# Routing records in rows of 512 bytes, and five small moves, in a mixture-of-experts kernel

## The chip, the cores and the metric

The kernel runs on one core of one Trainium2 chip. The metric is the device time of one execution in microseconds (us); less is better.

## The reference

The input x (4096 tokens of 512 numbers) is first rotated: each token is seen as four quaternion parts of 128 numbers, and the reference's filter and two Hamilton products come down to one 4x4 matrix per column of 128. Then comes a mixture of experts with 8 experts, 2 chosen for each token, and a capacity of 1024 slots for each expert:

```python
logits = xf @ gate_w.T
scores = softmax(logits);  topv, topi = top_k(scores, 2);  gates = topv / sum(topv)
# loc: the running number of the token among those that chose the same expert
valid = loc < cap                                  # cap = 1024
flat_idx = where(valid, topi * cap + loc, 0)
disp = zeros(E * cap, D).at[flat_idx].add(xf * w)
h = relu(einsum('ecd,ehd->ech', disp, fc1_w) + fc1_b)     # 512 -> 2048
eo = einsum('ech,ehd->ecd', h, fc2_w) + fc2_b             # 2048 -> 512
out = x + sum over the 2 choices of gathered(eo) * gates
```

All is float32.

## The kernel before

**Engines.** The kernel is written for each engine by hand: an instruction waits on semaphores, and each engine works through its own list in order. PE multiplies, ACT (ScalarE) and DVE (VectorE) prepare operands and take results, SP issues most DMAs on the hardware queue q1, POOL (GpSimd) issues plain and indirect DMAs on the software queue q0, and the same 16 DMA engines carry both queues.

**Routing.** The first 60 us load x (8 MB) into `x_all`, compute the logits, pick the experts and number the tokens. While this goes on, SP writes `x_all` to `out` (8 DMAs of 1 MB, semaphore `out_init`), since the experts' results are later added to rows of `out`; behind them, in the same queue, it loads W1 of group 1 (`load_w1(1)`). For expert 0 and 1 the token of each slot is found on chip (`find_tokens`, `read_slots`). For all others a table in DRAM, `table_dram`, says it: one row for each of 8192 slots, of which the first two numbers count (token number + 1, and its gate). POOL clears it (L398, from the tile `zeros`) once all of x has arrived, and later `scatter_records` (L472) writes 64 indirect DMAs of 128 records, each record a row of RECORD numbers. The records lie two numbers apart in the tile `records`, so a row also carries what follows its record; only its first two numbers are read back. The table is read with 8 DMAs (L518, semaphore `table_in`), and `read_table` (L1037 to L1042) turns it into `gather_row` and `scatter_row`; POOL waits for that (`tables_ready`) before it gathers the tokens of expert 2 and of later experts. `store_x` and `gather_x` bring token rows through `slots_dram`, and `cut_x` on SP reads them back cut in 32x32 blocks for DVE's transpose (`turn_x`).

**Products.** For each expert, groups g = 0..7 (G counts them over all experts) make 256 rows of h with seven products per group, a Strassen-like scheme on 2x2 blocks: A22, A11, A12, S1 to S4 are parts of W1 (high and low part `w1c_hi`, `w1c_lo`), B11, B21, T1 to T4, B22 parts of the rotated x (`yc_hi`, `yc_lo`). Each product is 6 matmuls of 128x512 (L1303 to L1305). Its result is picked up by ACT (`s2`, `s3`: L686, L702; `h_hi`: L725) and by DVE (`keep_c22` L1080, `keep_c12` L1086). `fc2(N)` (L1328, L1332, L1336) multiplies one tile of h with one tile of W2: 4 matmuls each of high x high, low x high, high x low. The last three tiles of all go through `fc2_end` (L1349 to L1351), one output block of 128 rows after the other; each block is added to `out` by DVE (`add_rows`) and written by POOL. The trace leaves numbers out of names: `s` is `s2` or `s3`, `w_raw` is `w1_raw` or `w2_raw`, `h` is `h1`.

**Ahead of the main loop** DVE's list runs: `turn_w1(1)` (two transposes at L816, which need both tiles of W1 of group 1), `read_slots(1)`, sums, `make_scores`, `w1_low_parts(1, 0)`, and then the rotation (`rotate_ps` from L1012 on), from which it works through to the first `keep_c22`. In ACT's list of group 0, `y_high` (L611) makes the high parts of T4 and B22, and L686 takes `s2` from the bank of the product S2 x T2; the product S3 x T3 adds into that bank, so PE waits for `s2_ready`.

Of the kernel before, what the change touches and what calls it, by code (L numbers as in the profile page):

```python
# [15 lines left out]
P = 128  # L16


def program(nc, x, cond, q_right, spectral, gate_w, fc1_w, fc1_b, fc2_w, fc2_b, out):
    B, S, D = x.shape  # L20
    E, H, _ = fc1_w.shape
# [23 lines left out]
    RECORD = 16  # L45
# [34 lines left out]
    with ctx:  # L80
        def sb(name, shape, dt=F32, where=ctx):
            return where.enter_context(nc.sbuf_tensor(name, shape, dt))
# [82 lines left out]
        zeros = sb("zeros", [P, E * CAP * RECORD // P], where=early)  # L165
# [88 lines left out]
        def version(N):  # L254

            e, n = N // STEPS, N % STEPS
            return e * VERSIONS + (n if n < HT else n - KEPT)
# [22 lines left out]
        def _(sp):  # L280
# [47 lines left out]
            for e in range(E):  # L328
                last = e == E - 1
                for g in range(GROUPS):  # L330
                    G, N = e * GROUPS + g, e * STEPS + 2 * g
                    if e and not last and g == 2:
                        cut_x(4 * e + 3)
                    if e and e < E - 2 and g == 5:
                        cut_x(4 * e + 4)
                    if e and e < E - 2 and g == 6:
                        cut_x(4 * e + 5)
                    load_w2(version(N) + 3)
                    load_w2(version(N) + 4)
                    if G + 3 < E * GROUPS:  # L340
                        load_w1(G + 3)
                    if G == 3:
                        cut_x(2)
                    if G == 4:
                        cut_x(3)
                    if G == GROUPS + 1:
                        cut_x(6)
# [12 lines left out]
        def _(pool):  # L360
# [37 lines left out]
            pool.dma_start(table_dram.rearrange("(p k) a -> p (k a)", p=P), zeros[:, :]).then_inc(table_cleared, 16)  # L398
# [146 lines left out]
        def _(act):  # L545
# [130 lines left out]
            for e in range(E):  # L676
                last = e == E - 1
                for g in range(GROUPS):
                    G, N = e * GROUPS + g, e * STEPS + 2 * g
                    odd_bias = b1T[:, e * HT + 2 * g + 1:e * HT + 2 * g + 2]  # L680
                    if e and g == 0:
                        seed_c11(G)
                    act.wait_ge(p6_done, G + 1)
# [3 lines left out]
                    if G == 0:  # L687
                        y_high(0, T4, 4, y21)
                        y_high(0, B22, 0, y22)
# [506 lines left out]
        def _(pe):  # L1196
# [111 lines left out]
            def fc2(N):  # L1308
# [21 lines left out]
                for b in range(SB):  # L1330
                    blk = slice(b * P, (b + 1) * P)
                    pe.matmul(eo_s[:, b, :], h_lo[:, c, blk], w2_hi[:, w, :], start=False, stop=False, skip_group_check=True)  # L1332
                pe.wait_ge(w2_ready, v + 1)
# [5 lines left out]
            def fc2_end(N):  # L1339

                eo_s = ps[:, EO[1]:EO[1] + SB, :]
                for b in range(SB):
                    blk = slice(b * P, (b + 1) * P)
                    for n in range(N, N + 3):
                        c, w = n % 3, version(n) % 3
                        if b == 0:
                            pe.wait_ge(w2_ready, version(n) + 1)
                            pe.wait_ge(h_ready, n + 1)
                        pe.matmul(eo_s[:, b, :], h_hi[:, c, blk], w2_hi[:, w, :], start=False, stop=False, skip_group_check=True)  # L1349
                        pe.matmul(eo_s[:, b, :], h_hi[:, c, blk], w2_lo[:, w, :], start=False, stop=False, skip_group_check=True)  # L1350
                        ins = pe.matmul(eo_s[:, b, :], h_lo[:, c, blk], w2_hi[:, w, :], start=False, stop=n == N + 2,  # L1351
                                        skip_group_check=True)
                    ins.then_inc(eo_done, 1)
# [44 lines left out]
            for e in range(E):  # L1398
                p1(e * GROUPS)
                p1(e * GROUPS + 1)  # L1400
                for g in range(GROUPS):
# [37 lines left out]
                    if g:  # L1439
                        fc2(N - 1)  # L1440
                    if G == 1:
                        p1(G + 1)
# [26 lines left out]
```

## Time and profile before

| | |
|---|---|
| median of 3 runs | 1439.35 us (1426.83 to 1447.98) |
| profiled execution, its own time | 1436.52 us |
| span of its instructions | 1434.6 us |
| PE busy | 1380.1 us (96%) |
| DVE, ACT, POOL busy | 1048.5, 701.8, 328.2 us |
| mean granted TensorE clock | 0.982 |

The span runs from the first to the last instruction of the profiled execution; its own time is 1.9 us more. A busy share is a mean over all stages. DMA issues, semaphore and register instructions count as idle, other than POOL's descriptor work.

### The profile page before, as it was taken

To read this page: it belongs to the slowest core of one execution; us is meant where nothing else is said; L and a number is where in the kernel's file an instruction comes from. 1 tells how busy PE (TensorE), PEld (TensorE's weight loads), DVE (VectorE), ACT (ScalarE), POOL (GpSimd) and SP (SyncE) were. 2 spreads that over 40 slices of the span, in tenths; PEclk is the share of its full clock that TensorE was granted. 3 is DMA by queue.
4 is the path that set the end of the run, shared out by engine and by line. 5 is a ranking of instruction groups with operands and counts; after the bars stand their busy time and mean duration, and the time that the engine had idled before them with its cause. 6 is when DMAs were issued, how large, how long until landed. Compare 5 with 4: busy or idle time off the path is not lost.

```text
span 1434.6 us, 18099 instructions
## 1 busy us (share of the span) xinstructions
PE 1380.1 (96%) x6159; PEld 1128.3 (79%) x6159; DVE 1048.5 (73%) x1580; ACT 701.8 (49%) x1056; POOL 328.2 (23%) x350
## 2 busy tenths in 40 slices
PE   8689779999999999999999999999999999999997
PEld 6477558788888888888888888888888888888885
DVE  6888449686886878777796878777786878855543
ACT  5465245454465445554555454654454554644442
POOL 1377751321033001221032010221032000220021
PEclk9799889999999999999999999999999999999999
DMA  8866434786465564565555564665555533543232
GB/s 316 292 137 143 75 82 110 208 192 141 97 177 162 108 138 115 157 170 135 95 169 158 106 151 92 184 162 121 114 151 151 128 74 74 146 125 67 52 98 78
DMA packets 450029, 195.36 MB, mean 136 GB/s; under 512 B 397641, under 2 KB 401922, under 8 KB 448146
## 3 DMA queue, kind: packets, MB, share of 16 engines
q1 hardware_dynamic: 427378, 125.98, 39.2%
q0 software_dynamic: 22560, 68.23, 14.8%
q8 instruction: 49, 0.80, 0.2%
q14 instruction: 42, 0.34, 0.1%
HBM read 153.51 MB, written 40.89 MB: 136 GB/s over the span
## 4 chain that ended last, share of the span: by engine, by line
PE 91%; another core or an unknown queue 3%; DVE 2%; issue 1%; DMA 1%; ACT 1%; SPq 0%; POOL 0%; DVEq 0%; ACTq 0%; POOLq 0%
PE ps L1332 14%; PE ps L1328 14%; PE ps L1336 14%; PE ps L1303 14%; PE ps L1305 14%; PE ps L1304 14%; PE ps L1239 1%; PE ps L1319 1%; PE ps L1321 1%; PE ps L1320 1%; PE ps L1294 1%; PE ps L1219 1%; PE ps L1220 1%; POOL h L412 0%
## 5 line engine op out<-in xcount | busy, mean ns | idle before, releaser
L1303 PE MATMUL ps<-yc_hi,w1c_hi 128*128 128x512 f32 x896 | 350.7, 391 | 14.8 <-issue 9.4
L1304 PE MATMUL ps<-yc_lo,w1c_hi 128*128 128x512 f32 x896 | 349.4, 390 | 0.0
L1305 PE MATMUL ps<-yc_hi,w1c_lo 128*128 128x512 f32 x896 | 349.2, 390 | 0.0
L1332 PE MATMUL ps<-w_hi,h_lo 128*128 128x512 f32 x952 | 255.9, 390 | 5.6 <-issue 5.6
L1336 PE MATMUL ps<-w_lo,h_hi 128*128 128x512 f32 x952 | 256.1, 390 | 1.6 <-issue 1.5
L1328 PE MATMUL ps<-w_hi,h_hi 128*128 128x512 f32 x952 | 254.8, 389 | 1.7 <-issue 1.7
L1332 PEld LDWEIGHTS ps<-w_hi,h_lo 128*128 128x128 f32 x952 | 178.9, 188 | 44.1 <-issue 6.8
L1336 PEld LDWEIGHTS ps<-w_lo,h_hi 128*128 128x128 f32 x952 | 179.1, 188 | 41.5 <-issue 4.5
L1303 PEld LDWEIGHTS ps<-yc_hi,w1c_hi 128*128 128x128 f32 x896 | 168.6, 188 | 54.7 <-issue 12.8
L1328 PEld LDWEIGHTS ps<-w_hi,h_hi 128*128 128x128 f32 x952 | 178.7, 188 | 37.9 <-issue 0.9
L1305 PEld LDWEIGHTS ps<-yc_hi,w1c_lo 128*128 128x128 f32 x896 | 168.6, 188 | 35.4
L1304 PEld LDWEIGHTS ps<-yc_lo,w1c_hi 128*128 128x128 f32 x896 | 168.6, 188 | 34.7
L951 DVE TENSOR_TENSOR w_lo<-w_raw,w_hi 128x512 fp32r<-128x512 f32 x232 | 158.4, 683 | 6.1 <-ACT w_hi L603 3.2
L945 DVE TENSOR_TENSOR w1c_lo<-w1t,w1c_hi 128x1792 fp32r<-128x1792 f32 x62 | 125.6, 2026 | 30.4 <-ACT w1c_hi L596 26.4
L603 ACT ACTIVATE w_hi<-w_raw 128x512 fp32r<-128x512 f32 x232 | 143.7, 620 | 7.0 <-DMA w_raw<-in_L_ffn_fc_w 7.0
L740 ACT ACTIVATE h_hi<-h 128x512 fp32r<-128x512 f32 x128 | 80.8, 631 | 131.6 <-PE ps L1336 107.5
L1030 DVE SCALAR_TENSOR_TENSOR h_lo<-ps,h_hi 128x512 fp32r<-128x512 f32 x64 | 44.1, 688 | 122.4 <-ACT h_hi L647 119.5
L596 ACT ACTIVATE w1c_hi<-w1t 128x1792 fp32r<-128x1792 f32 x62 | 105.7, 1706 | 52.8 <-DVE w1t L829 31.6
L1030 DVE SCALAR_TENSOR_TENSOR h_lo<-h,h_hi 128x512 fp32r<-128x512 f32 x128 | 88.4, 692 | 57.0 <-ACT h_hi L740 52.0
L1080 DVE SCALAR_TENSOR_TENSOR h<-ps,b1T,s 128x512 f32<-128x512 f32 x64 | 47.8, 746 | 92.7 <-PE ps L1305 87.0
L1000 DVE SCALAR_TENSOR_TENSOR yfull<-x_turned,rot,yfull 128x512 f32<-128x512 f32 x168 | 114.9, 747 | 0.0
L430 POOL DMA_INDIRECT x_blk<-in_x,gather_row x56 | 57.0, 1019 | 226.4 <-DVE x_turned L991 183.6
(189 smaller groups left out, 1482.9 us busy)
## 6 DMA issues: line engine op xcount, KB each, us to landing
w_raw<-in_L_ffn_fc_w SPq DMA_DIRECT2D x232, 256.0 KB
w_raw<-in_L_ffn_fc_w SPq DMA_DIRECT2D x512, 64.0 KB
slots_dram<-x_blk POOLq DMA_DIRECT2D x28, 512.0 KB
x_blk<-slots_dram SPq DMA_DIRECT2D x224, 64.0 KB
out<-x_all SPq DMA_DIRECT2D x8, 1024.0 KB, 13.1
x_all<-in_x SPq DMA_DIRECT2D x6, 1024.0 KB, 12.5
b_bc<-in_L_ffn_fc_b POOLq DMA_DIRECT2D x8, 256.0 KB
x_all<-in_x SPq DMA_DIRECT2D x4, 256.0 KB, 3.9
```

The source lines that it names most:

```text
L596: act.activation(w1c_hi[:, G % 2, :, :], w1t[:, 1:8, :], ACT.Copy).then_inc(w1_hi_ready, 1)
L603: act.activation(w2_hi[:, v % 3, :], w2_raw[:, v % 3, :], ACT.Copy).then_inc(w2_hi_ready, 1)
L945: dve.tensor_tensor(w1c_lo[:, G % 2, :, :], w1t[:, 1:8, :], w1c_hi[:, G % 2, :, :].bitcast(F32), ALU.subtract).then_inc(w1_ready, 1)
L951: dve.tensor_tensor(w2_lo[:, v % 3, :], w2_raw[:, v % 3, :], w2_hi[:, v % 3, :].bitcast(F32), ALU.subtract).then_inc(w2_ready, 1)
L1000: ins = dve.scalar_tensor_tensor(y, x_turned[:, :, j, :], rot[:, i, j:j + 1], y, ALU.mult, ALU.add)
L1030: dve.scalar_tensor_tensor(h_lo[:, N % 3, :], full, 0.0, h_hi[:, N % 3, :].bitcast(F32), ALU.max, ALU.subtract).then_inc(h_ready, 1)
L1303: pe.matmul(bank, hi, yc_hi[:, y, q, :], start=first and q == 0, stop=False, skip_group_check=True)
L1304: pe.matmul(bank, hi, yc_lo[:, y, q, :], start=False, stop=False, skip_group_check=True)
L1305: ins = pe.matmul(bank, lo, yc_hi[:, y, q, :], start=False, stop=last and q == 1, skip_group_check=True)
L1328: pe.matmul(eo_s[:, b, :], h_hi[:, c, blk], w2_hi[:, w, :], start=False, stop=False, skip_group_check=True)
L1332: pe.matmul(eo_s[:, b, :], h_lo[:, c, blk], w2_hi[:, w, :], start=False, stop=False, skip_group_check=True)
L1336: ins = pe.matmul(eo_s[:, b, :], h_hi[:, c, blk], w2_lo[:, w, :], start=False, stop=False, skip_group_check=True)
```

## The change

Six things change. (1) RECORD is 128 in place of 16: a record is a row of 512 bytes, and the table has 4 MB. `zeros` keeps its size, and the clearing DMA reads it 8 times. (2) SP issues `cut_x(3)` ahead of `load_w1(7)` in group 4, not behind it. (3) ACT makes the high parts of T4 and B22 ahead of `s2` in group 0, not behind it. (4) PE does the product `p1(2)` inside `fc2(1)`, ahead of its last four matmuls. (5) `fc2_end` begins with blocks 0 and 1 of its first two tiles, and only then waits for the third. (6) The tile `records` has 112 more columns, cleared once.

```diff
-    RECORD = 16
+    RECORD = 128
...
-        zeros = sb("zeros", [P, E * CAP * RECORD // P], where=early)
+        zeros = sb("zeros", [P, E * CAP * RECORD // P // NB], where=early)
...
+                    if G == 4:
+                        cut_x(3)
                     if G + 3 < E * GROUPS:
                         load_w1(G + 3)
                     if G == 3:
                         cut_x(2)
-                    if G == 4:
-                        cut_x(3)
...
-            pool.dma_start(table_dram.rearrange("(p k) a -> p (k a)", p=P), zeros[:, :]).then_inc(table_cleared, 16)
+            pool.dma_start(table_dram.rearrange("(p r k) a -> p r (k a)", p=P, r=NB),
+                           zeros[:, :].unsqueeze(1).to_broadcast([P, NB, E * CAP * RECORD // P // NB])).then_inc(table_cleared, 16)
...
+                    if G == 0:
+                        y_high(0, T4, 4, y21)
+                        y_high(0, B22, 0, y22)
                     act.wait_ge(p6_done, G + 1)
                     if G:
                         act.wait_ge(c12_done, G)
                     act.activation(s2[:, :], running(G), ACT.Copy).then_inc(s2_ready, 1)
-                    if G == 0:
-                        y_high(0, T4, 4, y21)
-                        y_high(0, B22, 0, y22)
...
-            def fc2(N):
+            def fc2(N, between=None):
...
+                if between is not None:
+                    p1(between)
                 pe.wait_ge(w2_ready, v + 1)
...
-                for b in range(SB):
-                    blk = slice(b * P, (b + 1) * P)
-                    for n in range(N, N + 3):
-                        c, w = n % 3, version(n) % 3
-                        if b == 0:
-                            pe.wait_ge(w2_ready, version(n) + 1)
-                            pe.wait_ge(h_ready, n + 1)
...
+                for n in (N, N + 1):
+                    pe.wait_ge(w2_ready, version(n) + 1)
+                    pe.wait_ge(h_ready, n + 1)
+                    add_step(n, 0)
+                for n in (N, N + 1):
+                    add_step(n, 1)
+                pe.wait_ge(w2_ready, version(N + 2) + 1)
+                pe.wait_ge(h_ready, N + 3)
+                for b in range(2):
+                    add_step(N + 2, b).then_inc(eo_done, 1)
+                for b in range(2, SB):
+                    add_step(N, b)
+                    add_step(N + 1, b)
+                    add_step(N + 2, b).then_inc(eo_done, 1)
...
-                        fc2(N - 1)
-                    if G == 1:
-                        p1(G + 1)
+                        fc2(N - 1, 2 if G == 1 else None)
```

ACT's list in group 0, around the evacuation `s2` (L686 before, L690 now; L611 and L612 are `y_high`, L702 and L703 `s3`). Before:

```order
L611 ACTIVATE yc_hi<-yfull 128x1024
L611 ACTIVATE yc_hi<-x_turned 128x1024
L611 ACTIVATE yc_hi<-yfull 128x1024
L686 ACTIVATE s2<-ps 128x512
L611 ACTIVATE yc_hi<-yfull 128x1024 x2
L702 ACTIVATE s3<-ps 128x512
```

Now:

```order
L612 ACTIVATE yc_hi<-yfull 128x1024
L612 ACTIVATE yc_hi<-x_turned 128x1024
L612 ACTIVATE yc_hi<-yfull 128x1024 x3
L690 ACTIVATE s2<-ps 128x512
L703 ACTIVATE s3<-ps 128x512
```

The two high parts of T4 and B22 stand ahead of `s2`, which waits behind them.

PE's list at the end of group 1, the step `fc2(1)` and the product `p1(2)`. Before:

```order
L1328 MATMUL ps<-w2_hi,h_hi 128x512 x4
L1332 MATMUL ps<-w2_hi,h_lo 128x512 x4
L1336 MATMUL ps<-w2_lo,h_hi 128x512 x4
L1303 MATMUL ps<-yc_hi,w1c_hi 128x512
L1304 MATMUL ps<-yc_lo,w1c_hi 128x512
```

Now:

```order
L1329 MATMUL ps<-w2_hi,h_hi 128x512 x4
L1333 MATMUL ps<-w2_hi,h_lo 128x512 x4
L1304 MATMUL ps<-yc_hi,w1c_hi 128x512
L1305 MATMUL ps<-yc_lo,w1c_hi 128x512
L1306 MATMUL ps<-yc_hi,w1c_lo 128x512
L1304 MATMUL ps<-yc_hi,w1c_hi 128x512
L1305 MATMUL ps<-yc_lo,w1c_hi 128x512
L1306 MATMUL ps<-yc_hi,w1c_lo 128x512
L1339 MATMUL ps<-w2_lo,h_hi 128x512 x4
```

The six matmuls of `p1(2)` stand four matmuls earlier.

SP's list of DMAs in group 4, as the difference of the two lists (`x_blk` is `cut_x(3)`, `w1_raw` is W1 of group 7, in 8 DMAs each):

```order
 L268 DMA x_blk<-slots_dram 32x16x32 x8
 L307 DMA w2_raw<-in_L0_ffn_fc2_w 128x512 x2
+L268 DMA x_blk<-slots_dram 32x16x32 x8
 L268 DMA w1_raw<-in_L0_ffn_fc1_w 32x16x32 x8
-L268 DMA x_blk<-slots_dram 32x16x32 x8
 L307 DMA w2_raw<-in_L0_ffn_fc2_w 128x512 x2
```

The cut rows of x go ahead of the weights of group 7.

## Rows read from the trace of the kernel before

**Rows 1.** The page's first part: busy time of each engine, share of the span, instructions.

```profile
PE 1380.1 (96%) x6159; PEld 1128.3 (79%) x6159; DVE 1048.5 (73%) x1580; ACT 701.8 (49%) x1056; POOL 328.2 (23%) x350
```

**Rows 2.** Stretches of the span, busy us (instructions) of each engine, clock, DMA.

```profile
core 0: us, PE busy (x) PEld busy (x) DVE busy (x) ACT busy (x) POOL busy (x), PEclk, DMA share, GB/s
151.00:200.00 49.00, 28.43 (x100) 20.04 (x99) 15.90 (x27) 9.28 (x14) 38.43 (x39) 0.76 0.29 48
200.00:249.00 49.00, 49.00 (x217) 40.23 (x216) 41.60 (x65) 26.78 (x39) 9.41 (x9) 1.00 0.53 129
290.00:1415.00 1125.00, 1125.00 (x4959) 930.08 (x4958) 833.72 (x1218) 564.71 (x838) 179.89 (x179) 1.00 0.53 129
```

**Rows 3.** Timeline of PE, 158 to 190 us; in brackets the idle time before.

```profile
161.07 0.39 PE L1305 MATMUL ps<-yc_hi,w1c_lo 128*128 128x512 f32 x1
...
187.23 0.79 PE L1303 MATMUL ps<-yc_hi,w1c_hi 128*128 128x512 f32 x1 [9.09 <-issue]
```

**Rows 4.** Timeline of ACT, 158 to 200 us.

```profile
161.15 0.69 ACT L725 ACTIVATE h_hi<-ps,b1T 128x512 fp32r<-128x512 f32 x1 [4.02 <-remote]
...
186.59 0.60 ACT L686 ACTIVATE s<-ps 128x512 f32<-128x512 f32 x1 [13.07 <-remote]
```

**Rows 5.** Timeline of POOL: the first scatter, the last long row, the table.

```profile
84.39 1.03 POOL L472 DMA_INDIRECT table_dram<-records,slot_row  x1 [0.30 <-issue]
...
137.82 1.01 POOL L472 DMA_INDIRECT table_dram<-records,slot_row  x1 [0.30 <-issue]
...
192.03 7.11 POOL L518 DMA_DIRECT2D table<-table_dram  x8 [1.43 <-DMA table_dram<-records,slot_row]
```

**Rows 6.** The same view of stretches, for the DMA load ahead of the main loop.

```profile
27.00:30.00 3.00, 3.00 (x22) 2.02 (x21) 2.54 (x4) 1.95 (x4) 0.76 (x1) 1.00 0.80 220
...
33.00:54.00 21.00, 9.57 (x60) 6.26 (x59) 16.96 (x38) 11.37 (x23) 4.02 (x7) 0.76 1.02 415
...
58.50:60.00 1.50, 0.85 (x17) 0.85 (x18) 1.50 (x2) 0.00 (x0) 1.18 (x1) 0.50 0.00 0
60.00:72.00 12.00, 10.80 (x50) 7.54 (x50) 11.53 (x30) 4.93 (x10) 9.30 (x10) 0.81 0.67 192
72.00:97.00 25.00, 21.71 (x89) 17.22 (x87) 23.76 (x35) 14.76 (x21) 20.89 (x25) 0.93 0.59 139
```

**Rows 7.** Timeline of POOL: the clearing of the table.

```profile
27.24 0.76 POOL L398 DMA_DIRECT2D table_dram<-zeros  x1 [20.97 <-DMA x_all<-in_x]
```

**Rows 8.** Timeline of SP, 50 to 68 us: the loads of W1 for group 1.

```profile
43.13 13.60 SPq L268 DMA_DIRECT2D w_raw<-in_L_ffn_fc_w  x6
```

**Rows 9.** Timeline of DVE ahead of the main loop.

```profile
60.26 1.30 DVE L816 STREAM_TRANSPOSE w1t<-w_raw 128x512 f32<-128x512 f32 x2
...
65.40 10.01 DVE L1012 SCALAR_TENSOR_TENSOR yfull<-ps,rot,yfull 128x256 f32<-128x256 f32 x24 [0.20 <-issue]
...
89.46 1.21 DVE L974 TENSOR_TENSOR yfull<-yfull 128x1024 f32<-128x1024 f32 x1
```

**Rows 10.** Timeline of ACT, 90 to 94 us.

```profile
90.83 0.60 ACT L686 ACTIVATE s<-ps 128x512 f32<-128x512 f32 x1 [1.81 <-PE ps L1305]
91.33 2.00 ACT L611 ACTIVATE yc_hi<-yfull 128x1024 fp32r<-128x1024 f32 x2
```

**Rows 11.** Timeline of PE, 91 to 95 us.

```profile
91.86 0.50 PE L1303 MATMUL ps<-yc_hi,w1c_hi 128*128 128x512 f32 x1 [0.28 <-issue]
...
94.31 0.47 PE L1303 MATMUL ps<-yc_hi,w1c_hi 128*128 128x512 f32 x1 [0.78 <-ACT s L702]
```

**Rows 12.** Timeline of PE, 111 to 115 us.

```profile
111.75 1.07 PE L1336 MATMUL ps<-w_lo,h_hi 128*128 128x512 f32 x4
...
114.93 0.50 PE L1303 MATMUL ps<-yc_hi,w1c_hi 128*128 128x512 f32 x1 [0.75 <-ACT ps L640]
```

**Rows 13.** Timeline of DVE, 235 us: the table is read.

```profile
235.57 0.19 DVE L1039 TENSOR_SCALAR slot_row<-table 128x64 f32<-128x64 f32 x1
```

**Rows 14.** Timeline of PE, the last steps.

```profile
1418.85 0.50 PE L1349 MATMUL ps<-w_hi,h_hi 128*128 128x512 f32 x1 [0.69 <-DVE w_lo L951]
```

More of the change, by code:

```diff
@@ L1341, in fc2_end, with add_step @@
                 eo_s = ps[:, EO[1]:EO[1] + SB, :]
-                for b in range(SB):
-                    blk = slice(b * P, (b + 1) * P)
-                    for n in range(N, N + 3):
-                        c, w = n % 3, version(n) % 3
-                        if b == 0:
-                            pe.wait_ge(w2_ready, version(n) + 1)
-                            pe.wait_ge(h_ready, n + 1)
[L1349 to L1353, printed above, removed]
+                def add_step(n, b):
+                    c, w, blk = n % 3, version(n) % 3, slice(b * P, (b + 1) * P)
+                    pe.matmul(eo_s[:, b, :], h_hi[:, c, blk], w2_hi[:, w, :], start=False, stop=False, skip_group_check=True)
+                    pe.matmul(eo_s[:, b, :], h_hi[:, c, blk], w2_lo[:, w, :], start=False, stop=False, skip_group_check=True)
+                    return pe.matmul(eo_s[:, b, :], h_lo[:, c, blk], w2_hi[:, w, :], start=False, stop=n == N + 2,
+                                     skip_group_check=True)
+                for n in (N, N + 1):
[12 more added lines that the diff above has]
+                    add_step(N + 2, b).then_inc(eo_done, 1)
             def set_bits(banks):
```

## The prediction

> **What bounds the kernel now.** I read the page's busy shares first: PE works for 1380.1 of 1434.6 us [rows 1]. The view of stretches says where the other 54.5 us lie. From 290 to 1415 us PE is busy for all 1125 us at full granted clock, 2.4 GHz; so the main loop and the second layer have nothing to give to any change that leaves the matmuls as they are, and this one has the same matmuls. What is not PE time lies ahead of 97 us, in the last 20 us, and in one hole: from 151 to 200 us PE has 100 matmuls, where the next 49 us have 217 [rows 2]. At 49/217 = 0.226 us each, 117 missing matmuls are 26.4 us.
>
> What is the hole? Its 38.43 us of POOL work are the clue: POOL issues the scatters of records 26 to 63 one behind the other from 137.8 us, with nothing between them, and the last has landed when the table's load starts at 192.0 us [rows 5]. The DMA engines are nearly empty in the hole (share 0.29, 48 GB/s [rows 2]), so it is no lack of bandwidth. PE is late in a strange way: the last matmul of group 4's S2 product starts at 161.1 us, but ACT, which needs nothing but that product and an h row, takes it at 186.6 us; ACT's earlier wait of 4.0 us has no known releaser either, and PE then stands idle for 9.1 us for what ACT makes [rows 3, 4]. That is a slow PE, or slow news from PE, and not a wait written in the code. It begins some 15 us into the unbroken row of scatters and is over when they are. Nothing else in the program is special to that stretch. So the 64-byte scatters are my suspect, by time alone; no row shows the mechanism.
>
> **The change part by part**, against the profiled execution's own span of 1434.6 us (its own time is 1.9 us more, 1436.5, and 2.8 us under the median of 1439.35).
>
> *Rows of 512 bytes, the hole.* The number of scatters (64) and of rows in each (128) stays; the bytes of a scatter go from 8 to 64 KB. The bounds: the hole is gone (-26.4 us), or it stays as it is (0), or grows (a rival below). I take -26.4: the gathers of 2048-byte rows ahead of the loop (60 to 72 us, ten of them, as densely issued) go by with PE busy for 10.8 of 12 us [rows 6], so descriptors from POOL alone don't make a hole; what is special in the scatters is that they write small rows.
>
> The Trainium skill bears on this in "DMA: Bandwidth & Descriptors", section Specifications: a transfer under 512 B makes the DMA engine read, modify and write. By that rule the new rows shed the extra read; it doesn't say that PE would notice, and no row here shows it. The sum would be the same by it.
>
> *Rows of 512 bytes, the scatters' own load.* 56 KB more for each of 64 scatters is 3.7 MB over some 105 us, 35 GB/s beside loads that take a DMA share of 0.5 to 0.6. POOL's issue time goes by rows, not bytes (38.43 us for 39 instructions in the hole, 9.30 for 10 gathers of 2048-byte rows [rows 2, 6]), so 0, as long as the table is in time: its last load is issued at 199.1 us and DVE reads it at 235.6 [rows 5, 13]. With the hole gone DVE comes at 209, and POOL and DVE both come later by the next term; some 10 us of cover are left. If each of 64 scatters took 0.16 us longer, that would be used up; the spacing in the long row is now (190.6 - 137.8) / 38 = 1.39 us.
>
> *The clearing.* It is issued at 27.2 us [rows 7] with 4 MB in place of 0.5: 3.67 MB more, while SP's queue is full. From 33 to 54 us the DMA engines are saturated at 415 GB/s [rows 6], so everything behind is late by 3.67 MB / 415 GB/s = 8.8 us, less what was free from 27 to 30 us (share 0.80: 0.6 us), 8.2 us. What is behind: the writes of `out`, and in the same queue the 8 loads of W1 for group 1, the last of which is issued by 56.7 us and landed by 58.5 us, when DMA traffic is 0 [rows 6, 8]. Now they end at 66.7 us, and they meet the gathers of expert 0's rows (share 0.67 [rows 6]), for which I add 2 us: 68.7 us. DVE turns the second tile at 60.9 us (half of the pair of 1.30 us from 60.26) and the rotation begins 4.5 us later, at 65.4 [rows 9]. After that DVE is busy for 23.76 of the 25 us up to 97 us [rows 6], so its start sets everything: 68.7 + 4.5 = 73.2 in place of 65.4, **+8 us**. The bounds: +5 (no loss to the gathers and some more overlap) and +11 (the gathers win every turn). It would be 0 only if the 16 engines had more than 415 GB/s to give, and the rows don't show that.
>
> The logits are ahead of this: W1 of group 0 lands in the same stretch as the clearing, and DVE, in order, may lose 2 to 4 us on it near 31 us. That lies under the 8 us, since routing and W1 of group 1 meet only at `read_slots(1)`.
>
> The Trainium skill prices the same thing in "DMA: Bandwidth & Descriptors", section "Anatomy of one DMA — SWDGE (gpsimd) path": about 2.0 us plus bytes/436e3, so an estimate of 8.4 us for 3.67 MB more, where the row gives 8.8; the sum would be 0.4 us less.
>
> *ACT's order in group 0.* The high part of T4 waits for DVE's difference, done at 90.7 us [rows 9]; two high parts take 2.0 us, so `s2` starts at 92.7 in place of 90.8 [rows 10]. PE's S3 product, which waits for it, then starts at about 93.4 in place of 91.9, and A22 1.5 us later as well, in place of 94.3 [rows 11]. DVE gets the high parts earlier and saves 0.6 us that don't bind any more. PE's first step of group 1 comes **+1.2 us** later, after what it now waits for DVE. Bounds: 0 to +1.5.
>
> *p1(2) earlier.* In group 2 PE waits 0.75 us for ACT, whose step waits for `p1(2)` [rows 12]. Four matmuls earlier are 0.9 us: **-0.75**, and 0 if DVE's high parts of W1 are late.
>
> *fc2_end.* The third tile is waited for 0.69 us [rows 14]; six matmuls (1.4 us) now fill that. Block 3 is the last in both orders: **-0.7**.
>
> *cut_x(3) first.* 8 DMAs change places with 8 others. Behind them on SP are W2 loads, unchanged. W1 of group 7 comes that much later: it is issued in group 4 and turned in group 5, and a group is 66 matmuls or 14.9 us. In a full queue six such DMAs took 13.6 us [rows 8], so eight would take 18 and cost up to 3 us; the DMA engines are half free here (share 0.53 in the next stretch [rows 2]), so I take none. The cut rows come earlier, and `turn_x(3)` stands early in DVE's group 5, so without the hole the old order might have made DVE wait. So 0, between -2 and +3.
>
> The sum: -26.4 + 8 + 1.2 - 0.75 - 0.7 = -18.7 us. Span 1416.0, own time **1418 us**, 1.5% under the median.
>
> **Rivals.**
>
> *A, the forecast.* 1418 us; with the bounds of the clearing and ACT 1413 to 1422. Chance 0.56.
>
> *B, the hole stays.* It comes with the number of rows or with POOL's unbroken descriptor work, neither of which the change touches. For it: scatters run from 84.4 us [rows 5], and from there to 137.8 us, in rows of at most ten, they open no such hole, so the length of a row may be what counts and not what it writes. Against it: the gathers. 1434.6 + 8 + 1.2 - 1.45 + 1.9 = 1444 us, 0.3% over the median. Chance 0.23. A hole of half the size gives 1431 us, chance 0.08.
>
> *C, slower.* The hole comes with the bytes that small scattered rows write. Then eight times the bytes make it begin with the unbroken row at 137.8 and not at 151 us: 14 us more at the mean loss of the hole (26.4 of 39 us), so 9.5 us more; and the ten scatters in a row behind `store_x(1)`, 14 us, would show the same loss, 9.5 us again. Price: 1444 + 19 = 1463 us. It decides from the point where PE loses over 21.4 us in all to such holes (1439.35 - 1418); it passes 2% only if the table is late as well. Chance 0.08, a good half of it over 2%.
>
> *D, the clearing is hidden.* If out's writes give way instead of W1's loads, the start of the rotation moves by less than 3 us: 1410 us. Chance 0.05.
>
> **How the numbers follow.** A measurement of this kernel can tell about 2% from no change: under 1410.6 us is faster, over 1468.1 slower. A and D are mostly within; but the median of before moves by 10 us from run to run (1426.8 to 1448.0), perhaps with the length of the hole, and A's time would stand at 2% under the highest of them. So faster 0.18, same 0.75, slower 0.07. The range takes A, B, the half-size hole and D, each with the outer part of its own spread cut, and leaves out C, under 2 in 10 in all: 1406 to 1446.
>
> **What would show it.** Right: between 137 and 200 us of the new trace PE has no stretch under its full rate, and ACT's steps there have PE as releaser. The clearing: the last W1 load of group 1 at 66 to 71 us, DVE's first rotation at 71 to 76. The ACT term: `s2` of group 0 behind two high parts, PE idle ahead of S3 by about 1.8 us. The tail: no wait ahead of the last third of tiles. The forecast is wrong if the hole stays (B, C), or if the table comes late: then DVE waits at its read of the table, and POOL's next gathers with it.

## The result, and the profile after

The changed kernel took **1440.09 us** (median of 20 runs, 1433.83 to 1447.88); beside it, on the same chip, the kernel before took 1430.49 (20 runs, 1418.71 to 1447.98). The ratio is 1.008, 95% interval [1.006, 1.010]: a small loss that twenty runs can tell, where I had forecast a gain of 1.5%. Medians, here and below, are over all runs, but the ratios leave out a few runs in a slower state, so a ratio need not be the quotient of its two medians. The profiled execution of the changed kernel took 1437.52 us, span 1435.5.

First the same stretches as in [rows 2], and PE's busy share:

```profile
PE 1381.1 (96%) x6159; PEld 1128.6 (79%) x6159; DVE 1049.0 (73%) x1580; ACT 702.0 (49%) x1056; POOL 327.2 (23%) x350
```

```profile
151.00:200.00 49.00, 42.03 (x171) 32.86 (x170) 26.07 (x42) 13.60 (x19) 38.33 (x36) 0.93 0.61 137
200.00:249.00 49.00, 45.61 (x186) 35.80 (x187) 38.77 (x59) 26.57 (x39) 19.14 (x21) 0.93 0.49 108
290.00:1415.00 1125.00, 1125.00 (x4958) 930.04 (x4958) 835.33 (x1220) 565.94 (x839) 180.63 (x180) 1.00 0.54 129
```

The main loop is what it was. The hole is still there, later and shorter: over the two stretches 357 matmuls against 317, so 40 x 0.226 = 9 us less is lost. ACT's waits in it have no known releaser: for 9.56 us it waits for nothing that the trace shows, for 6.35 us for something that it doesn't know, as in [rows 4]. The hole is over when POOL's row is, as in [rows 5]. Timelines of ACT, then of POOL:

```profile
193.73 0.66 ACT L641 ACTIVATE ps<-ps,b1T 128x512 f32<-128x512 f32 x1 [9.56 <-issue]
200.74 0.69 ACT L726 ACTIVATE h_hi<-ps,b1T 128x512 fp32r<-128x512 f32 x1 [6.35 <-remote]
```

```profile
29.17 1.07 POOL L398 DMA_DIRECT2D table_dram<-zeros  x1 [22.79 <-DMA x_all<-in_x]
...
205.63 7.11 POOL L519 DMA_DIRECT2D table<-table_dram  x8 [1.55 <-DMA table_dram<-records,slot_row]
```

What the hole gives back is taken at the start. The timeline of DVE (L817 is the turn of W1, L1013 the rotation) answers to [rows 9], that of PE to the stretch ahead of it, and the page's DMA part gives the clearing's time from issue to landing, 14.4 us:

```profile
29.88 0.71 DVE L817 STREAM_TRANSPOSE w1t<-w_raw 128x512 f32<-128x512 f32 x1 [0.64 <-DMA w_raw<-in_L_ffn_fc_w]
40.88 0.71 DVE L817 STREAM_TRANSPOSE w1t<-w_raw 128x512 f32<-128x512 f32 x1 [9.12 <-DMA w_raw<-in_L_ffn_fc_w]
...
71.73 1.30 DVE L817 STREAM_TRANSPOSE w1t<-w_raw 128x512 f32<-128x512 f32 x2
76.59 10.00 DVE L1013 SCALAR_TENSOR_TENSOR yfull<-ps,rot,yfull 128x256 f32<-128x256 f32 x24
```

The second of these turns in the kernel before:

```profile
31.30 0.71 DVE L816 STREAM_TRANSPOSE w1t<-w_raw 128x512 f32<-128x512 f32 x1 [0.45 <-DMA w_raw<-in_L_ffn_fc_w]
```

```profile
42.23 0.61 PE L1220 MATMUL ps<-xT_hi,grot_hl 128*16 128x512 f32 x1 [8.03 <-DVE xT_lo L845]
```

```profile
table_dram<-zeros POOLq DMA_DIRECT2D x1, 4096.0 KB, 14.4
```

W1 of group 1 is no trouble: its turn at 71.73 has no wait. It is the second tile of W1 of group **0**, 9.12 us late, that stops DVE in the middle of cutting x for the logits; PE waits behind it for `xT_lo`, and the routing, and the rotation with it, start 11.2 us later (76.59 against 65.40). One profile of each would be thin, but the experiments below bear it out: with the clearing of 4 MB in this place the rotation starts at 76.6 to 79.6 us in four traces, with 512 KB at 65.4 to 70.1 in thirteen.

Around the first group, ACT and then PE, which answer to [rows 10, 11]:

```profile
101.76 2.01 ACT L612 ACTIVATE yc_hi<-yfull 128x1024 fp32r<-128x1024 f32 x2 [1.80 <-DVE yfull L975]
103.67 0.58 ACT L690 ACTIVATE s<-ps 128x512 f32<-128x512 f32 x1
```

```profile
104.39 0.47 PE L1304 MATMUL ps<-yc_hi,w1c_hi 128*128 128x512 f32 x1 [1.95 <-ACT s L690]
```

`s2` stands behind the two high parts, and PE waits 1.95 us for it, as drawn.

### The profile page after: what moved, and what is told of

It is laid out like the page before. It is cut to its first block, busy times and chain, and to the rows that moved or that the text cites. A ratio compares the mean times of both kernels' runs of the same rounds, so it can differ in the third digit from the quotient of the medians.

```text
span 1435.5 us, 18098 instructions
## 1 busy us (share of the span) xinstructions
PE 1381.1 (96%) x6159; PEld 1128.6 (79%) x6159; DVE 1049.0 (73%) x1580; ACT 702.0 (49%) x1056; POOL 327.2 (23%) x350
## 4 chain that ended last, share of the span: by engine, by line
PE 88%; DVE 3%; SPq 2%; another core or an unknown queue 2%; issue 2%; DMA 1%; ACT 1%; POOL 0%; DVEq 0%; ACTq 0%; POOLq 0%
PE ps L1333 14%; PE ps L1339 14%; PE ps L1329 14%; PE ps L1304 14%; PE ps L1306 13%; PE ps L1305 13%; SPq L268 2%; DMA w_raw<-in_L_ffn_fc_w 1%; PE ps L1320 1%; PE ps L1321 1%; PE ps L1322 1%; DVE yc_lo L979 0%; DVE yfull L1026 0%; DVE w_lo L952 0%
## 5 line engine op out<-in xcount | busy, mean ns | idle before, releaser
L703 ACT ACTIVATE s<-ps 128x512 f32<-128x512 f32 x64 | 38.3, 598 | 144.3 <-PE ps L1306 133.9
## 6 DMA issues: line engine op xcount, KB each, us to landing
table_dram<-zeros POOLq DMA_DIRECT2D x1, 4096.0 KB, 14.4
```

## The experiments

Kernels were measured in series: each series on one chip, with runs of the kernel before between them. The expectations call a series a call. The time of the kernel before is not the same in all of them, and that is the main finding:

```
series                   kernel before, median us (lowest to highest)
the changed kernel       1430.5 (1418.7 to 1448.0)
1: e1 to e4              1438.7 (1422.7 to 1452.4)
2: e5 to e8              1440.1 (1423.5 to 1455.1)
3: e9 to e12             1409.9 (1408.1 to 1412.6)
4: e13 to e16            1410.5 (1408.1 to 1415.3)
5: e17, e18              1430.3 (1419.3 to 1448.2)
```

Series 1, 2 and 3 ran on a chip of the same number, series 4 and 5 on two others.

### Series 1: the parts of the change, and no scatters

**e1**, the long rows and the clearing of 4 MB alone, in the kernel before:

```diff
-    RECORD = 16
+    RECORD = 128
```

> The kernel before with the 512-byte rows and the 4 MB clearing alone; all other moves undone. Theory now (clearing costs ahead of the loop, hole in the row of scatters gets shorter but stays): the second tile of W1 of group 0 lands near 41 us and DVE waits some 9 us for it, the rotation starts near 76.6 us in place of 65.4, and the whole is 0.6 to 1.0% slower than before. Rival (the slowdown comes from the moved steps of ACT, PE and SP): within 0.2% of before.

1451.44 us, 1.007 [1.004, 1.011]. Stretches (from here on of PE alone: busy us, matmuls, clock, DMA share, GB/s), and DVE:

```profile
151.00:200.00 49.00, 42.32 (x184) 1.00 0.60 139
200.00:249.00 49.00, 41.79 (x168) 0.86 0.43 90
```

```profile
44.55 0.71 DVE L817 STREAM_TRANSPOSE w1t<-w_raw 128x512 f32<-128x512 f32 x1 [11.18 <-DMA w_raw<-in_L_ffn_fc_w]
```

The hole is there with 512-byte rows, and so is DVE's wait for W1 of group 0. The whole loss of the change comes with this part.

**e2**, the other four edits alone (the changed kernel with `RECORD = 16` and the old clearing):

> The changed kernel with 64-byte rows and the clearing of 0.5 MB again, all moved steps kept. Theory: the rotation starts at 65 to 66 us; ACT's order costs 1.3 us, the product and the last steps give 1.4 us back, so within 0.2% of before, with a hole of some 20 to 27 us under the scatters as before. Rival (moves are the loss): 0.6% or more slower than before.

1440.8 us, 1.001 [0.998, 1.004]; 94 matmuls from 151 to 200 us, the hole of the kernel before.

**e3**, the kernel before with no scatter of records at all (the table stays empty, so the second layer's weights are left out):

```diff
-                for c in columns:
+                for c in ():
```

> The kernel before without its 64 scatters of records (left out: the table stays empty, so the experts from 2 on all take token 0 and add nothing to the output). Theory (POOL's scatters make the hole): PE has its full 217 or so matmuls in every 49 us from 115 to 290 us, and the time is 15 to 27 us shorter, 1.1 to 1.9% faster. Rival (the hole comes from something else at that place, such as instruction fetches or SP's loads): a hole of 15 us or more stays between 150 and 210 us and the time is within 0.5% of before.

1412.01 us, 0.981 [0.976, 0.986], and its runs lie within 3.8 us where those of the kernel before lie within 30.

```profile
151.00:200.00 49.00, 47.27 (x209) 1.00 0.44 85
200.00:249.00 49.00, 49.00 (x216) 1.00 0.60 147
```

No hole. So the scatters are needed for it, and the spread of the kernel before from run to run goes with the hole.

**e4**, the changed kernel with the clearing issued behind the gathers of expert 0's rows, and waited for ahead of the first scatter:

```diff
             gather_x0(range(2 * SB))
+            pool.dma_start(table_dram..., zeros...).then_inc(table_cleared, 16)
```

> The changed kernel with the 4 MB clearing issued behind the 8 gathers of expert 0's rows (from a tile of 512 bytes per partition read 64 times) and waited for ahead of the first scatter. Theory (the clearing's price is its place): DVE's wait for W1 of group 0 is under 1 us again, the rotation starts by 67 us, and the time is 6 to 11 us under the changed kernel's, 0 to 0.3% around or under before. Rival (the 4 MB cost the same wherever they are, since x blocks and W1 of group 2 wait for them next): within 0.2% of the changed kernel.

1448.11 us, 1.008 [1.005, 1.012]: as much as the changed kernel, so the rival holds, the 4 MB cost the same here. W1 of group 0 was in time and the rotation started at 66.3 us. What ate the gain up is not the hole alone: PE already does only 181 matmuls from 100 to 151 us, where e2 has 226, and waits 5.1 us for weights at 120.6, which e16 shows better. Its profiled execution, 1462.4 us, is the longest of its twelve runs, so the depth of the hole in it says little of the median:

```profile
100.00:151.00 51.00, 43.49 (x181) 0.97 0.76 180
151.00:200.00 49.00, 17.41 (x47) 0.64 0.29 74
```

### Series 2: what about the scatters makes the hole

**e5**, the clearing behind W1 of group 0:

```diff
+            for t in range(2):
+                pool.wait_ge(w1_in[t], 16 * W1_DMAS)
             pool.dma_start(table_dram..., zeros...).then_inc(table_cleared, 16)
```

> The changed kernel, with POOL waiting for both tiles of W1 of group 0 before it issues the clearing of 4 MB. Theory (the clearing costs only because it shares the DMA engines with W1 of group 0, which delays the logits and the rotation behind them by 11 us): DVE's turn of W1 of group 0 waits under 2 us again, the rotation starts near 66.5 us, and the time is that of the run with the moves only, 0.995 to 1.004 of before. Rival (the 4 MB cost the same wherever they lie, as when the clearing was issued behind the gathers of x0): 1.006 to 1.011, with the rotation at 66 us and a hole under the scatters that has grown to over 30 us. Second rival: the clearing then collides with W1 of group 1 (58.5 us before): DVE's turn of it waits 3 to 8 us, 1.002 to 1.005.

1447.18 us, 1.005 [1.002, 1.007]. Timelines of POOL and DVE:

```profile
67.46 0.95 POOL L415 DMA_INDIRECT h<-in_x,gather_row  x1 [14.64 <-DMA rows<-in_x,part_i]
```

```profile
68.46 0.71 DVE L819 STREAM_TRANSPOSE w1t<-w_raw 128x512 f32<-128x512 f32 x1 [8.11 <-DMA w_raw<-in_L_ffn_fc_w]
72.27 0.71 DVE L819 STREAM_TRANSPOSE w1t<-w_raw 128x512 f32<-128x512 f32 x1 [3.10 <-DMA w_raw<-in_L_ffn_fc_w]
```

The second rival: the ratio is at the upper end of its 1.002 to 1.005, and the waits, 11.2 us together, are more than its 3 to 8. The price has moved. The clearing, issued at 32.6 us, now takes 33.5 us to land; POOL waits 14.64 us for a gather of its own queue, issued at 51.7 us, and so the gathers of x0 are late; and W1 of group 1 is 11 us late. That is the path that I had predicted for the clearing where it stood.

**e6**, the last 38 scatters replaced by 38 gathers of 64-byte pieces of x into an idle tile (these records are left out):

```diff
-            scatter_records(range(26, TOPK * TJ))
+            for c in range(26, TOPK * TJ):
+                pool.indirect_dma_start(slab_rows[0][..16 elements..], None, x_pieces, ...)
```

> The kernel before, in which the last 38 scatters of records are replaced by 38 gathers of as many pieces of 64 bytes from x into an idle tile (the table then lacks these records, so the results of their tokens are left out). Theory 1 (the hole is made by POOL issuing an unbroken row of indirect DMAs, whatever they move): the stretch from 151 to 200 us still lacks over 80 of 216 matmuls, and the time stays within 0.5% of before. Theory 2 (the hole is made by what scatters alone do, writes of single small rows to memory and their completions): the stretch holds over 190 matmuls and the time is 0.978 to 0.987 of before, as without scatters.

1439.13 us, 0.999 [0.995, 1.002]:

```profile
151.00:200.00 49.00, 22.39 (x79) 0.66 0.32 45
```

Theory 1, clearly: nothing is written to DRAM in this row, and the hole is as deep as ever.

**e7**, a wait for all that was issued, ahead of every third scatter from number 30 on:

```diff
                 for c in columns:
+                    if c > 29 and c % 3 == 0:
+                        pool.wait_ge(records_out, 16 * c)
```

> The kernel before, in which POOL waits in the last row of 38 scatters, ahead of every third of them, until all that it issued have landed. Theory 1 (many indirect DMAs in flight at once delay the semaphores and transfers of the others): the row lasts 80 to 110 us in place of 53, its end near 230 us, but the hole shrinks to under 8 us, and the time is 0.982 to 0.992 of before. Theory 2 (each scatter costs the others its share, in flight or not): the lost time is the same, spread over the longer row, 0.996 to 1.004. Rival 3: the table is now late for VectorE's reading of it (235.6 us before), and the time rises to 1.005 to 1.015.

1432.52 us, 0.997 [0.994, 0.999], its runs within 4.6 us. PE's stretches, and DVE at its read of the table:

```profile
151.00:200.00 49.00, 47.29 (x209) 1.00 0.48 91
200.00:249.00 49.00, 30.65 (x127) 0.79 0.39 93
```

```profile
233.25 0.20 DVE L1041 TENSOR_SCALAR slot_row<-table 128x64 f32<-128x64 f32 x1 [18.27 <-DMA table<-table_dram]
```

The mechanisms of theory 1 and of rival 3 at once, so the time lies between their ranges: under the row PE is at its full rate, with the same scatters; but the row now ends at 223 us, and DVE waits 18.27 us for the table. One hole went and another, this one plainly written in the program, took its place.

**e8**, the last 19 scatters left out (and their records):

```diff
-            scatter_records(range(26, TOPK * TJ))
+            scatter_records(range(26, 45))
```

> The kernel before with the last 19 of 64 scatters left out (their records are missing from the table, so their tokens' results are left out too). The last row is then 19 scatters, some 25 us, from 138 to 163 us. Theory 1 (a hole opens only once a row has lasted some 25 us, here at 161 us, and lasts until the row ends): no hole, the stretch from 151 to 200 us holds over 200 matmuls, time 0.979 to 0.986 of before. Theory 2 (each scatter costs the same 0.4 us or so of the others' time): 19 of 64 scatters' share of 27 us, 8 us, is gained: 0.993 to 0.996. Rival 3 (the end of the row is what is waited for): the hole lies earlier and is shorter by 25 us: as theory 1.

1415.08 us, 0.982 [0.978, 0.987], with 209 matmuls from 151 to 200 us. Leaving out 30% of the scatters removes all of the hole, not 30% of it: in this series a row of 19 makes none, where the row of 38 in e6 lost PE 32 us.

### Series 3: pauses, in a series without the hole

**e9** (the kernel before), **e10** (the changed kernel) and **e11** (the four moves) got waits ahead of three scatters, **e12** (the kernel before) ahead of one:

```diff
                 for c in columns:
+                    if c in (36, 46, 56):     # e12: if c in (45,)
+                        pool.wait_ge(records_out, 16 * c)
```

> The kernel before, in which POOL waits at three places in the last row of 38 scatters (ahead of numbers 36, 46 and 56) until all that it issued have landed. Theory (a hole needs a row of over some 20 indirect DMAs without a pause): no hole, 151 to 200 us holds over 200 matmuls; the three waits of 2 to 4 us make the row end near 203 us, before VectorE wants the table (214 us), so nothing is late: 0.980 to 0.986 of before. Rival (it was the rate of one scatter in 1.3 us over the whole row, which waits at every third brought down to one in 2.1): half of the hole or more stays, 0.990 to 0.998.

> The changed kernel with the same three waits. With no hole to absorb it, the 11 us by which the clearing of 4 MB delays the start, and the 1 us of ACT's new order, less 0.8 us at the end, show in full: 1420 to 1427 us, 0.986 to 0.992 of before, 9 to 12 us above the kernel before with the waits. Rival (the delay of the start is taken back elsewhere): within 3 us of the kernel before with the waits.

> The changed kernel with rows of 64 bytes and a clearing of 512 KB again (the four moves alone), with the same three waits. The moves are worth 0.8 us at the end and some 0.5 at p1(2), and cost 1.3 us at ACT: 0.980 to 0.986 of before, within 2 us of the kernel before with the waits. Rival (with the hole gone the moves show a gain or a loss of their own): 3 us or more on either side of it.

> The kernel before with one such wait only, in the middle of the row (ahead of number 45), so that two rows of 19 are left. Theory (a backlog grows with the row's length and is cleared by any pause): as with 19 scatters left out no hole opens, 0.980 to 0.987. Rival (the pause must be longer or come more often): a hole of 5 to 15 us in the second half, 0.987 to 0.995.

1413.21 us (1.002 [1.001, 1.003]), 1425.0 (1.010 [1.009, 1.012]), 1415.0 (1.004 [1.003, 1.006]) and 1409.57 (1.000 [0.999, 1.000]). All had their full rate under the row, but so had the kernel before: at 1409.9 us it was 30 us under series 2 with no edit. So e9 and e12 say nothing on pauses, and the ratios expected of them, which were against a kernel with the hole, were missed for that reason. What stands is the pair e10 and e9: 11.8 us between the changed kernel and the kernel before, of which DVE's wait for the table, pushed back by the pauses, is a part (4.28 us, and 1.17 in e9):

```profile
223.12 0.20 DVE L1042 TENSOR_SCALAR slot_row<-table 128x64 f32<-128x64 f32 x1 [4.28 <-DMA table<-table_dram]
```

e11 against e9 is the only pair of the four moves without the hole. It lies within the 2 us expected, but by its median (five runs) it is 1.8 us slower than e9, while its profiled execution, the fastest of the five, is 2.6 us faster.

### Series 4: both kernels again, word for word

> The kernel before, word for word. In the call with the pauses the kernel before itself ran in 1408 to 1413 us, 25 to 30 below its times of all other calls, so the hole was absent there without any edit. Theory 1 (the hole comes and goes with something outside the kernel, from call to call): the time is near 1410, with over 200 matmuls from 151 to 200 us, or near 1430 to 1440, with under 120, and the other kernels of this call follow suit. Theory 2 (that call was of a kind that does not come back): near 1435 with the hole.

> The changed kernel, word for word. If this call has no hole, the delay of the start is not absorbed and it is 1.007 to 1.009 of before, near 1421 us (the pair with the pauses differed by 11.8 us, and the waits cost the changed kernel some 2 by a late table). If it has the hole: 1.005 to 1.010, near 1440.

**e13**, the kernel before: 1410.34 us, 1.000 [0.999, 1.001]. Its stretches:

```profile
151.00:200.00 49.00, 47.85 (x211) 1.00 0.48 89
200.00:249.00 49.00, 49.00 (x216) 1.00 0.78 204
```

Compare [rows 2]: the same program, the same 38 scatters in a row (POOL is busy for 38.52 us of the 49), and 111 matmuls more. **e14**, the changed kernel: 1419.27 us, **1.005** [1.004, 1.007], 218 and 216 matmuls in these stretches. That is a little less than the 1.007 to 1.009 expected of it.

```profile
42.87 0.71 DVE L817 STREAM_TRANSPOSE w1t<-w_raw 128x512 f32<-128x512 f32 x1 [11.38 <-DMA w_raw<-in_L_ffn_fc_w]
```

**e15**, e9 once more:

> The kernel before with the three waits in the last row of scatters, as measured before. Where the hole is there: theory (a pause clears the backlog) 0.980 to 0.986 of before; rival (the pauses did nothing and the call had no hole to begin with) 0.995 to 1.004. Where it is absent: 1.001 to 1.003 again, which tells nothing.

1414.03 us, 1.002 [1.001, 1.004], which tells nothing, as the expectation says.

**e16**, e4 with one pause (ahead of number 45):

> The changed kernel with the clearing of 4 MB behind the gathers of x0, and one pause in the middle of the last row. Without a hole: if the 4 MB are free there (the fetches that they meet have slack), 0.998 to 1.003 of before; if they cost the same wherever they lie, 1.006 to 1.010. With a hole: the pause should take it away, 0.980 to 0.990, or the hole stays and it is 1.005 to 1.012.

1419.89 us, 1.007 [1.004, 1.009], as expected if the 4 MB cost the same wherever they lie. Without the hole one sees what the late clearing costs. Timelines of POOL, ACT and PE:

```profile
93.81 0.82 POOL L440 DMA_DIRECT2D slots_dram<-x_blk  x1 [9.29 <-DMA x_blk<-in_x,gather_row]
```

```profile
116.95 0.63 ACT L607 ACTIVATE w_hi<-w_raw 128x512 fp32r<-128x512 f32 x1 [8.46 <-DMA w_raw<-in_L_ffn_fc_w]
```

```profile
121.28 0.79 PE L1307 MATMUL ps<-yc_hi,w1c_hi 128*128 128x512 f32 x1 [7.53 <-DVE w1c_lo L949]
```

The weights of the main loop's first groups are late behind it, and PE loses 7.5 us at once, and some more because the next matmuls follow each other at 0.43 us and not at 0.23: the granted clock is 0.50 from 121 to 125 us. In three places, beside W1 of group 0, behind it, and behind x0, the 4 MB bring waits of 7.5 to 11.4 us.

### Series 5: the moves alone

> The four moves alone (rows of 64 bytes, clearing of 512 KB), as in the first run of this kernel. Without the hole: the earlier cuts of x for version 3 take away TensorE's wait of 1.15 us near 172 us, p1(2) some 0.9 near 115, the last steps 1.0 at the end, and ACT's order costs 0.4: 0.997 to 0.999 of before, near 1407 us, and so the clearing and rows of 512 bytes cost the changed kernel 12 us, not 9. Rival (what the moves gain is given back before the end): 1.000 or more. With the hole: 0.998 to 1.004.

> The same without the move on ACT (s2 of group 0 ahead of the two high parts again), so three moves. If ACT's order costs what TensorE waits more for s2 and S3 there (1.95 and 0.78 against 0.78): 1 to 1.3 us below the run with four moves. Rival (the parts of y21 and y22 were wanted as early, and the order costs nothing): within 0.5 us of it.

**e17** (the kernel of e2) 1428.0 us, 1.000 [0.998, 1.003]; **e18**, without the move on ACT, 1428.43, 0.999 [0.996, 1.001]. The hole was back (139 matmuls from 151 to 200 us in both), and the spread from run to run, 7 to 8 us, covers the 1 us between the two expectations. The order on ACT can't be told from nothing by time.

## Why the prediction was wrong

**The step that failed** is "*Rows of 512 bytes, the hole*", where I took -26.4 from the bounds -26.4 and 0. The runs give 0 in place of it, as far as the scatter of the profiles lets one tell: e1 and the changed kernel have the hole with 512-byte rows, 17 to 19 us in their profiles, and e17 and e18 have one of 18 us with 64-byte rows. e6 has it with a row that writes nothing to DRAM, and e8 has 45 of the 64 scatters and no hole. By e8 and e7, where the hole is to be had at all, what counts is how long POOL issues indirect DMAs without a break, and the change doesn't touch that. I had this in rival B, "in rows of at most ten, they open no such hole", and let ten gathers outweigh it; but ten gathers are also a row of at most ten, so they spoke for neither side. The measured 1440.09 us are B's case. That they are only 4 us from its 1444 is in part luck: B started from the median of three runs, 9 us above that of twenty, and had the clearing 3 to 4 us too cheap.

The Trainium skill's rule that a transfer under 512 B is a read, a change and a write ("DMA: Bandwidth & Descriptors", section Specifications) may well hold; no run here shows it in a time.

**A wrong premise lies under it.** I took the hole for a property of the kernel. e13 shows the kernel before without it. Nor is it the scatters alone: they are needed for it (e3, e8), but in two of six series the full row leaves PE at its rate. The chip alone doesn't decide it either: series 1 and 2 have the hole and series 3 has not, on a chip of the same number. What goes with the kind of series is the number of semaphore changes that the trace of the profiled execution holds, counted in the traces:

```
kernel           series with  records in all  150 to 190 us
before           the hole     20627            114
after            the hole     20831            265
e6 (gathers)     the hole     20730            110
e7 (waits)       the hole     21064            620
e8 (half row)    the hole     20639            518
e13 (before)     no hole      24201           1092
e14 (after)      no hole      24255           1242
```

The same program leaves 3574 records fewer in a series with the hole, and where POOL issues its row about one in ten is left (in part because PE does half the work there). That would explain why ACT's waits there have no known releaser ([rows 4]). Loss and hole aren't the same: e7 and e8 lose as many in all and have no hole, so a loss alone doesn't bring it; with a long row PE stands still as well. Every time here comes with a span and a granted clock, so I take each to be of an execution that was recorded. It is my reading, and only that, that the recording is what can't keep up in those series and holds the engines back.

On this the Trainium skill has a rule, in "NOTIFIC — the notification-queue block", section "Overflow: three behaviours, one of which stalls the engine": inside the block that writes such records none is lost, those who make them are held back instead, which could throttle an engine; when the ring in memory is full, a setting decides whether records are dropped or their maker stands still. Together that would fit records that are missing and an engine that slows while the row lasts; no run without recording is there to show it, and the hole might as well have a cause that also loses records.

**The clearing** was +8 us, bounds +5 to +11, by way of W1 of group 1. It was +11.2 in the profile after [rows 9], and +11.7 in e14 against e13 (the rotation starts at 77.86 and 66.13 us), and it went by the path that I had written off. DVE waits for W1 of group 0 not "2 to 4 us" but 9.1 to 11.4 (0.5 and 2.4 in `before` and e13), and that doesn't lie under the term; it is the term, since the delayed logits move everything behind them. When the clearing was moved away (e4, e5, e16) this wait was gone. The failure is that I charged the load issued last: W1 of group 0, in flight together with the clearing, is turned only 11.7 us after the clearing's issue, with the DMA engines full from 31 to 41 us (share 1.03).

**The other terms**, by the time at which the k-th matmul starts (the first is 0), counted in the traces without the hole:

```
k        417    480    550    700    760    1000   4000    6158
e13      89.5  106.3  123.1  157.1  172.1  226.9  908.0  1398.6
e14     101.5  118.3  134.3  168.3  181.9  236.6  917.5  1407.1
more     12.0   12.0   11.2   11.2    9.8    9.7    9.5     8.5
```

- ACT's order: predicted +1.2. The wait of 1.95 us for `s2` is in the profile after, but in e14 that wait is 0.49 us, and against e13 nothing is left of it at matmul 480. e18 could not tell it either. At most 0.5 us.
- `p1(2)`: predicted -0.75. Between 480 and 550: -0.8.
- `cut_x(3)`: predicted 0, between -2 and +3. Between 700 and 760: -1.4. It is the wait that I had named as possible. Timelines of DVE and PE in e13; in e14 neither waits there:

```profile
169.80 1.30 DVE L991 STREAM_TRANSPOSE x_turned<-x_blk 128x512 f32<-128x512 f32 x2 [5.28 <-DMA x_blk<-slots_dram]
```

```profile
171.79 0.50 PE L1303 MATMUL ps<-yc_hi,w1c_hi 128*128 128x512 f32 x1 [1.15 <-DVE h L1080]
```

- `fc2_end`: predicted -0.7. From 4000 to the end: -1.0. In e13 the wait of [rows 14] stands again; in e14 it is gone.

```profile
1391.88 0.50 PE L1349 MATMUL ps<-w_hi,h_hi 128*128 128x512 f32 x1 [0.69 <-DVE w_lo L951]
```

So without the hole the sum is +12 - 0.8 - 1.4 - 1.0 - 0.3 = +8.5 us (the 0.3 lie between 760 and 4000, and I ascribe them to nothing), against 8.9 between the medians (1419.27 and 1410.34). With the hole it was 9.6 (1440.09 and 1430.49). Between the two profiled executions there is only 1.0 us (1437.52 and 1436.52), since the start was 11.2 later and the hole 9 us shorter; but the 64-byte rows of e17 had as short a hole, and one profile of each can't say that it shrank in the mean.

One slip of the text: the product whose last matmul starts at 161.1 us is group 5's S2, not group 4's. Nothing hangs on it.

**What stays open.** What differs between the series with and without the hole; whether an execution that isn't recorded has it; whether three pauses take it away (e9 and e15 fell in series without it; only e7, with twelve, is shown). Whether p1, `cut_x(3)` and `fc2_end` alone beat the kernel before: the table, of one profile each, gives some 3 us, but e18 gives 0.999 [0.996, 1.001], no more than a hint, and e11's median speaks against it. The only kernel with its full output that is faster than the kernel before by more than its interval is e7, by 0.3%, and only where the hole is.

## What to carry to other kernels

Before a term is built on a stretch in which engines wait for nothing that the trace knows, run the unchanged kernel again, in another series if that is to be had: what comes and goes there is no property of the program. A big transfer that is put into a saturated stretch must be charged first to the load that is in flight with it and whose consumer stands in order ahead of the critical chain, and only then to the last one of the queue; and moving it is no gain by itself, here it cost about the same in two other places. A comparison with a short row of DMAs says nothing about a long one.

## What the runs showed of the hardware

- A row of 38 indirect DMAs of POOL, 1.3 us apart, cost PE 17 to 32 us in the profiles of four series (26 in the kernel before; 44 in e4's, its longest run), with 64-byte rows 18 to 28, with 512-byte rows 17 to 29, with gathers of 64-byte pieces 32; in one of these series 19 in a row, or three at a time with waits of 1.9 to 4.5 us between, made no hole. In two series the row of 38 cost nothing either.
- The kernel before spread over 29 to 32 us in a series with the hole, over 5 to 7 in one without. Every kernel without the hole stayed within 3 to 7 us, but so did e17 with it (7).
- A clearing of 4 MB took 14.4 us and one of 512 KB 3.5. By the Trainium skill's fit for such a transfer ("DMA: Bandwidth & Descriptors", section "Anatomy of one DMA — SWDGE (gpsimd) path") they would take an estimated 11.6 and 3.2 us; that is near for the small one. The big one ran beside W1 and the writes of `out`, and in other places it took 33.5 us (e5) and 21.0 (e16), so its time went by what it met.
- POOL's issue time for a scatter was the same with 8 KB and with 64 KB: 0.98 to 1.2 us for most, 2.2 at most.
